# Summing the thresholds of an FP4 quantiser with separate compares and adds, two of the adds on GpSimd

## The reference

```python
scale = max(max|xb| / 6, 1e-12)          # over a block of 16 values
idx = searchsorted(_MID, |xb / scale|)   # _MID: 0.25 0.75 1.25 1.75 2.5 3.5 5.0
q = _GRID[idx] * sign(xb) * scale        # _GRID: 0 0.5 1 1.5 2 3 4 6
h = silu(xq @ wgq.T) * (xq @ wuq.T)      # 1024 -> 2816
ffn = quant(h) @ wdq.T                   # 2816 -> 1024
```

## Time and profile before

| | |
|---|---|
| median of 3 runs | 14323.8 us (14305.8 to 14346.3) |
| the profiled execution | 14373.7 us |
| its span, slowest core (core 5) | 14372.0 us |
| spans of the eight cores | 14229.1 to 14372.0 us |
| mean granted TensorE clock, cores 0 to 3, 4 to 7 | 0.652, 0.643 of full speed |
| busy on core 5: TensorE, VectorE, ScalarE, GpSimd | 45%, 51%, 18%, 10% |
| VectorE, stage 3 after its weights | busy 2979 of 4400 us |

### The profile page before, as it was taken

The page is one execution under the profiler, slowest core; times in us unless marked ns, Lnnn a source line. Parts: engine busy times, 40 slices in busy tenths (PEclk is TensorE's granted clock), DMA queues, the critical chain, the costliest instruction groups (busy, mean ns, idle before and its releaser), DMA issues.

```text
span 14372.0 us, 115863 instructions; the slowest of 8 cores (14229.1 to 14372.0 us)
## 1 busy us (share of the span) xinstructions
PE 6406.0 (45%) x27434; PEld 2691.4 (19%) x27434; DVE 7295.3 (51%) x19406; ACT 2554.8 (18%) x3860; POOL 1501.5 (10%) x1616
## 2 busy tenths in 40 slices
PE   1444444444545555554554003344334333440577
PEld 1111111111222222222221001111111111110233
DVE  4333334443444434434445986666666666668300
ACT  2222222222222222222222111111111111111000
POOL 1111111110000000000001111111111111111000
PEclk8777777776655555565555556666666666665677
DMA  2111111101100010010010000000000000001233
GB/s 61 42 42 42 37 41 39 39 34 49 46 26 28 30 42 25 28 46 26 28 46 23 30 31 11 11 21 12 11 11 22 11 11 22 11 9 37 100 111 110
DMA packets 285008, 505.41 MB, mean 35 GB/s; under 512 B 35506, under 2 KB 207410, under 8 KB 282306
## 3 DMA queue, kind: packets, MB, share of 16 engines
q1 hardware_dynamic: 235842, 333.82, 7.3%
q0 software_dynamic: 48512, 164.18, 3.0%
HBM read 294.17 MB, written 199.81 MB: 34 GB/s over the span
## 4 chain that ended last, share of the span: by engine, by line
PE 26%; issue 25%; DVE 23%; DMA 13%; ACT 9%; SPq 2%; DVEq 1%; ACTq 0%; POOL 0%; POOLq 0%
PE p_d L1603 4%; PE p_u L1480 4%; DMA s_siluz<-stg_ev 4%; DMA s_xbc<-stg_ev 4%; DVE q_s L305 3%; PE p_g L1471 2%; PE p_sc L1370 2%; ACT q_sg L257 2%; PE p_seg L1370 2%; DMA hqt<-s_hqT 2%; DVE hb L1500 1%; PE ptrA L372 1%; DVE q_s L323 1%; DVE q_amax L275 1%; ACT q_absx L256 1%
## 5 line engine op out<-in xcount | busy, mean ns | idle before, releaser
L1480 PE MATMUL p_u<-wut,xq 128*128 128x512 bf16 (+1 forms) x3072 | 842.7, 430 | 1649.1 <-DVE hb L1500 1649.1
L345 POOL TENSOR_TENSOR q_ss<-q_sg,q_sclh 128x512 f16<-128x512 f16 (+3 forms) x560 | 787.7, 1424 | 5400.3 <-DVE q_rcp L285 5200.4
L678 PE MATMUL pmm<-xhT,wnt 128*128 128x512 bf16 (+1 forms) x4352 | 1078.4, 392 | 207.8 <-ACT stg_ev L695 205.4
L305 DVE SCALAR_TENSOR_TENSOR q_s<-q_aa,q_s 128x512 f16<-128x512 f16 (+3 forms) x1680 | 975.4, 646 | 0.3 <-DVE q_s L299 0.3
L1603 PE MATMUL p_d<-wdt,hqt 128*128 128x512 bf16 x2816 | 763.8, 446 | 200.4 <-DVE ostg L1617 199.5
L1471 PE MATMUL p_g<-wgt,xq 128*128 128x512 bf16 (+1 forms) x3072 | 796.9, 409 | 26.9 <-ACT gs L1492 18.7
L1492 ACT ACTIVATE gs<-p_g 128x512 bf16<-128x512 f32 (+1 forms) x384 | 213.0, 555 | 3272.1 <-DVE hb L1500 1858.8
L724 DVE COPY dtstg<-pmm 16x512 f32<-16x512 f32 x16 | 10.8, 678 | 1437.7 <-PE pmm L683 1437.7
L1480 PEld LDWEIGHTS p_u<-wut,xq 128*128 128x128 bf16 x3072 | 337.7, 113 | 2093.4 <-issue 1863.9
L1187 DVE SCALAR_TENSOR_TENSOR attb<-eb,ldtT,scoresM 128x256 bf16<-128x256 bf16 x1024 | 455.1, 485 | 498.3 <-ACT eb L1173 428.5
L1500 DVE TENSOR_TENSOR hb<-p_u,gs 128x512 f32<-128x512 f32 (+1 forms) x384 | 246.7, 642 | 873.5 <-PE p_u L1480 873.3
(11 more groups left out here) (218 smaller groups left out, 12810.4 us busy)
## 6 DMA issues: line engine op xcount, KB each, us to landing
s_hqT<-hqTb POOLq DMA_DIRECT2D x16, 2816.0 KB, 11.5
hqt<-s_hqT SPq DMA_DIRECT2D x16, 2816.0 KB
xbcw<-s_xbc SPq DMA_DIRECT2D x272, 128.8 KB
s_xbc<-stg_ev SPq DMA_DIRECT2D x272, 128.0 KB
ubuf<-u SPq DMA_DIRECT2D x16, 2048.0 KB
s_siluz<-stg_ev POOLq DMA_DIRECT2D x256, 128.0 KB, 2.0
zld<-s_siluz SPq DMA_DIRECT2D x16, 2048.0 KB
ubp<-u SPq DMA_DIRECT2D x64, 512.0 KB
```

What stands on the lines that cost most here:

```text
L305: vop(f"t{k}", i, nc.vector.scalar_tensor_tensor(q["s1"][:, CS[i]], q["aa"][:, CS[i]], QTHR[k], q["s1"][:, CS[i]], ALU.is_gt, ALU.add))
L345: ii = nc.gpsimd.tensor_mul(q["ss"][:, CS[i]], q["sg"][:, CS[i]], q["sclh16"][:, GS[i]].unsqueeze(2) .broadcast_to([128, hb, 16]))
L678: nc.tensor.matmul(pm[0:rows, :], wnt[:, k * F + ft * 128: k * F + ft * 128 + rows], xhT[:, k * TILE:(k + 1) * TILE], start=(k == 0), stop ...
L1480: i = nc.tensor.matmul(p_u[:, 0:nn], xqb[:, k * TILE + mt * 128: k * TILE + (mt + 1) * 128], wut[:, k * FFI + i0: k * FFI + i1], start=(k ...
```

## The change

Three new scratch tiles `cd`, `c5`, `c6`. The compare-and-add instructions go: each threshold is now compared on its own (a tensor-scalar instruction, `is_gt` then a multiplication by the weight 1, 2 or 4), and added by a plain tensor-tensor add. The adds of thresholds 2 to 4 and the last one (`fin`) are on VectorE; the two that gather `s2`, `c5` and `c6` are on GpSimd, in two halves, four instructions per call. VectorE waits for them before `fin`. Also, ScalarE's `absx` and `sg` of the next call now wait for the last `aa` and the last `ss` of the call before, in place of its end.

```diff
             if q.get("prev") is not None:
-                w(scalar, "ve", q["prev"])
-                w(scalar, "gp", q["prev_gp"])
+                w(scalar, "ve", q["prev_absx"])
+                w(scalar, "gp", q["prev_sg"])
...
-            for k in (1, 2, 3):
-                for i in (0, 1):
-                    vw(mk[(f"t{k-1}", i)])
-                    vop(f"t{k}", i, nc.vector.scalar_tensor_tensor(
-                        q["s1"][:, CS[i]], q["aa"][:, CS[i]], QTHR[k],
-                        q["s1"][:, CS[i]], ALU.is_gt, ALU.add))
...
+                vop("c0", i, nc.vector.tensor_scalar(
+                    q["cc"][:, CS[i]], q["aa"][:, CS[i]], QTHR[1], 1.0,
                     ALU.is_gt, ALU.mult))
...
+                vop("t1", i, nc.vector.tensor_add(
+                    q["s1"][:, CS[i]], q["s1"][:, CS[i]], q["cc"][:, CS[i]]))
+                vop("c1", i, nc.vector.tensor_scalar(
...
+                vop("t2", i, nc.vector.tensor_add(
...
+                vop("c2", i, nc.vector.tensor_scalar(
...
+            for i in (0, 1):
+                vw(mk[("t2", i)])
+                vw(mk[("c2", i)])
+                vop("t3", i, nc.vector.tensor_add(
+                    q["s1"][:, CS[i]], q["s1"][:, CS[i]], q["cc"][:, CS[i]]))
+                vop("u0", i, nc.vector.tensor_scalar(
+                    q["s2"][:, CS[i]], q["aa"][:, CS[i]], QTHR[4], 2.0,
+                    ALU.is_gt, ALU.mult))
+                vop("u1", i, nc.vector.tensor_scalar(
+                    q["c5"][:, CS[i]], q["aa"][:, CS[i]], QTHR[5], 2.0,
+                    ALU.is_gt, ALU.mult))
+                vop("u2", i, nc.vector.tensor_scalar(
+                    q["c6"][:, CS[i]], q["aa"][:, CS[i]], QTHR[6], 4.0,
                     ALU.is_gt, ALU.mult))
             for i in (0, 1):
                 vw(mk[("t3", i)])
...
+                nc.vector.wait_ge(sems["gp"], gp_ad[i])
+                vop("fin", i, nc.vector.tensor_add(
+                    q["s1"][:, CS[i]], q["s1"][:, CS[i]], q["s2"][:, CS[i]]))
             for i in (0, 1):
-                vw(mk[("v2", i)])
-                nc.vector.wait_ge(sems["gp"], gp_ss[i])
+                vw(mk[("fin", i)])
                 vop("ds", i, nc.vector.tensor_mul(
                     dst[:, CS[i]], q["s1"][:, CS[i]], q["ss"][:, CS[i]]))
...
+            for i in (0, 1):
+                gpsimd.wait_ge(sems["ve"], mk[("u2", i)])
+                ii = nc.gpsimd.tensor_add(
+                    q["s2"][:, CS[i]], q["s2"][:, CS[i]], q["c5"][:, CS[i]])
+                inc(ii, "gp")
+            for i in (0, 1):
+                gpsimd.wait_ge(sems["gp"], gp0 + 3 + i)
+                ii = nc.gpsimd.tensor_add(
+                    q["s2"][:, CS[i]], q["s2"][:, CS[i]], q["c6"][:, CS[i]])
+                inc(ii, "gp")
```

More of the change, by code:

```diff
@@ L233, in quant_scratch @@
             "cc": sb(f"{tag}_cc", [128, n], F16 if f16 else BF16),
+            "cd": sb(f"{tag}_cd", [128, n], F16 if f16 else BF16),
+            "c5": sb(f"{tag}_c5", [128, n], F16 if f16 else BF16),
+            "c6": sb(f"{tag}_c6", [128, n], F16 if f16 else BF16),
             "ss": sb(f"{tag}_ss", [128, n], F16 if f16 else BF16),
@@ L259, in emit_quant_full @@
         AC = cnt["ac"]
-        gp_ss = [cnt["gp"] + 1, cnt["gp"] + 2]
+        gp0 = cnt["gp"]
+        gp_ss = [gp0 + 1, gp0 + 2]
+        gp_ad = [gp0 + 5, gp0 + 6]
         mk = {}
@@ L273, in _ @@
                 vw(q["prev"])
+                nc.vector.wait_ge(sems["gp"], q["prev_gp"])
             for i in (0, 1):
@@ L301, in _ @@
                     ALU.is_gt, ALU.mult))
-            for k in (1, 2, 3):
-                for i in (0, 1):
-                    vw(mk[(f"t{k-1}", i)])
-                    vop(f"t{k}", i, nc.vector.scalar_tensor_tensor(
-                        q["s1"][:, CS[i]], q["aa"][:, CS[i]], QTHR[k],
-                        q["s1"][:, CS[i]], ALU.is_gt, ALU.add))
-            for i in (0, 1):
-                vop("u0", i, nc.vector.tensor_scalar(
-                    q["s2"][:, CS[i]], q["aa"][:, CS[i]], QTHR[4], 1.0,
+                vop("c0", i, nc.vector.tensor_scalar(
+                    q["cc"][:, CS[i]], q["aa"][:, CS[i]], QTHR[1], 1.0,
@@ L311, in _ @@
                     ALU.is_gt, ALU.mult))
             for i in (0, 1):
[L313 to L318, removed]
+                vw(mk[("t0", i)])
+                vw(mk[("c0", i)])
+                vop("t1", i, nc.vector.tensor_add(
+                    q["s1"][:, CS[i]], q["s1"][:, CS[i]], q["cc"][:, CS[i]]))
@@ new lines, in _ @@
+                vop("c1", i, nc.vector.tensor_scalar(
+                    q["cd"][:, CS[i]], q["aa"][:, CS[i]], QTHR[2], 1.0,
+                    ALU.is_gt, ALU.mult))
+            for i in (0, 1):
+                vw(mk[("t1", i)])
+                vw(mk[("c1", i)])
+                vop("t2", i, nc.vector.tensor_add(
+                    q["s1"][:, CS[i]], q["s1"][:, CS[i]], q["cd"][:, CS[i]]))
+                vop("c2", i, nc.vector.tensor_scalar(
+                    q["cc"][:, CS[i]], q["aa"][:, CS[i]], QTHR[3], 1.0,
+                    ALU.is_gt, ALU.mult))
@@ L349, in _ @@
                 inc(ii, "gp")
-        assert cnt["gp"] == gp_ss[1]
+            for i in (0, 1):
[3 more added lines that the diff above has]
+                inc(ii, "gp")
+            for i in (0, 1):
+                gpsimd.wait_ge(sems["gp"], gp0 + 3 + i)
+                ii = nc.gpsimd.tensor_add(
+                    q["s2"][:, CS[i]], q["s2"][:, CS[i]], q["c6"][:, CS[i]])
+                inc(ii, "gp")
+        assert cnt["gp"] == gp0 + 6
         q["prev"] = cnt["ve"]
         q["prev_gp"] = cnt["gp"]
+        q["prev_absx"] = mk[("aa", 1)]
+        q["prev_sg"] = gp_ss[1]
         return cnt["ve"]
```

## The result

The changed kernel takes 14743.4 us (median of 8 runs, 14711.4 to 14787.0), the kernel before beside it 14334.7: ratio 1.0288, 95% interval 1.0266 to 1.0309. That is slower by 409 us; the forecast was +387 us, 2.7%, in a range of 14480 to 15020.

A forecast was written before the change was run, and what follows sets the result against it. Bound: one chain through VectorE, 324 quantisation calls in full. Calls +444 us and ScalarE's earlier release -57 give +387, on a 14324 us median: 14711 us, range 14480 to 15020.

The forecast's parts named there:

- One chain through VectorE: Quantisation calls: waits in stage 3 are for work VectorE itself releases, so all 324 calls count in full.
- Rival D: The call's growth is partly covered, for instance by TensorE in stages 1 and 3; half covered 14490; chance 0.05.
- The saving: VectorE, each f16 call: 8.0 us removed, 5.1 added; alone saves 2.9 us, about 740 us over 256 calls.
- T: 1,024-column f16 call: when the first half's `u2` is done, forecast 3.56 us from the first L305's old place.
- the mark: Zero point for timing a call: where the first L305, a compare, stood in the old order.
- The wait: VectorE held by GpSimd's adds before `fin`; f16 call 9.93 against 8.77 us, +1.15; narrow +1.10, weight +2.25.
- The price of an add: GpSimd add taken as 1.05 us for 512 columns, 0.83 for 384; bounds 0.95 to 1.22.
- Whoever waits gets in as the other ends: Turn-taking of VectorE and GpSimd instructions that don't overlap, read from the earlier trace; GpSimd's add enters after `t3`.
- Rival A: VectorE and GpSimd do overlap: +0.39 us per f16 call, +1.07 per f32, 14440 in all; chance 0.05.
- rival C: A plain GpSimd add is much cheaper than a product with a broadcast operand; at 0.60 us 14153; chance 0.03.
- rival B: Each GpSimd add lasts 1.49 us: +545 us more, 15256; chance 0.05.
- The release: ScalarE released earlier: VectorE waits less in stage 1 and the weight stages, nothing in stage 3; together -57 us.

The follow-up runs named there:

- first experiment: The changed kernel with the four GpSimd adds of each call moved to VectorE; 0.9712 of the kernel before.
- extra-adds run: Kernel with all adds on VectorE, plus four GpSimd adds per f16 call into an unread scratch tile; 1.0342 of the kernel before, against 0.9712 without them.
- reordered one: The changed kernel with the three high-threshold compares (u0, u1, u2) moved in front of the low ones; 1.0203 of the kernel before.
- two-adds run: The changed kernel with two of the four GpSimd adds of a call (those of c6) moved to VectorE; 1.0005 of the kernel before.

## Why the prediction was right

**The bound.** One chain through VectorE, every call in full: stage 3 grew by 239 us. The calls as measured there give 128x1.36+64x1.13 = 246, so hardly anything was covered (on core 3 VectorE's wait for `p_u` fell from 870.6 to 849.2 us). Rival D is out.

**The saving.** The pitches held: compare 0.20, plain add 0.335 (starts at 11208.37 and 11208.70). T, the end of the first half's `u2`, came 3.57 us behind the mark, 3.56 forecast. The first experiment shows the saving without GpSimd: 0.9712, 0.968 expected.

**The wait.** From T to the end of the call 6.56 us, 6.37 forecast; the call +1.36 against +1.15; the narrow call +1.13 (11247.61 to 11255.68) against +1.10; the weight call 11.74 us (8321.10 to 8332.84) against 11.55, +2.44 where 2.25 was forecast. In these two the mark is again set behind the start of the first compare as in the old order (0.99 and 1.52 us); for the weight call, by its first compare and its products:

```profile
8319.58 1.27 DVE L305 TENSOR_SCALAR qw_s<-qw_aa 128x512 bf16<-128x512 f32 x1
...
8332.09 0.75 DVE L348 TENSOR_TENSOR wbf<-qw_s,qw_ss 128x512 bf16<-128x512 bf16 x2
```

**Two steps in it were off.** The price of an add was taken as 1.05 and measured 1.14 us (0.83 and 0.90 for 384 columns), within the bounds that I gave (0.95 to 1.22). The last three adds run from 11210.36 to 11213.72, 3.36 us in place of 3.15, and that is all of the 0.19 us. And the order at T was not the one chosen. I had GpSimd get in after `t3` and hold the second half's compares until T+1.78. In the trace they run freely to T+0.94, and GpSimd's first add, started at T+0.14, ends only at T+1.94, some 1.0 us behind the last of them. That is one of the prediction's own signs of being wrong ("if `t3` and the compares don't get held"), and the other order that it named and priced at 0.1 us. It was worth almost nothing: GpSimd's second add starts at T+1.91, T+1.93 forecast (T+1.49 and 1.56 in the narrow call, T+2.31 and 2.34 in the weight call), since in either order the compares and the add stand one behind the other. VectorE's idle time before `fin` is 3.32 us in place of about 2 for the same reason. "Whoever waits gets in as the other ends" is not general. It is what happens in the extra-adds run and in the reordered one, but not behind this `t3`, nor in the two-adds run, where GpSimd waits through six VectorE instructions. What decides who gets in first was not settled.

**Exclusion.** Argued from the earlier trace rows, shown by the experiments from the reordering on. Rival A (14440) and rival C fell with them and with the first; rival B's 1.49 us is not the work of an add: L370, with VectorE out of the way, has a mean of 1143 ns, and only L365, whose first add has to wait, one of 1469.

**The release.** -57 us forecast, 52 less idle time in the trace, 27 +/- 29 us by the runs: compatible with both. The share of it in stage 1 (12.7 us less idle time) does not show in the length of that stage.

**The sum.** With the measured calls it would be 192x1.36+64x1.13+68x2.44-52 = +447 us. The lengths of the stages bear that out (us, median of the eight cores in the two traces):

| | before | after | growth | forecast |
|---|---|---|---|---|
| stage 1, first block maximum to last product | 2896.4 | 2979.9 | 83.5 | 61 |
| gate and up weights, first block maximum to first `hb` | 788.5 | 883.7 | 95.2 | 89 |
| stage 3, first to last `hb` | 4346.1 | 4584.9 | 238.8 | 218 |
| down weights, first block maximum to last product | 408.8 | 432.3 | 23.5 | 20 |

That is 441 us where 388 was forecast: every stage grew by more than its forecast, by 53 us together. The runs' medians differ by 409 (interval 381 to 443). They are times of the slowest core, and which core that is hangs in part on the down projection, which the change leaves alone and which took 885 to 977 us on the cores before and 881 to 967 after; in the two profiled executions the slowest core grew by 379 us and the median core by 444. So 387 came nearer to 409 than its steps deserved, and that part is luck. The 32 us between 441 and 409 have no cause that I tested.

## What to carry to other kernels

Moving elementwise work from VectorE to GpSimd did not relieve VectorE here: each GpSimd add took some 0.9 us out of VectorE's time, waited for or not, while the same work on VectorE was 0.335 us for an add and 0.60 for a product. This held beside tensor-scalar, tensor-tensor and scalar-tensor-tensor instructions; no trace here has a reduction, a reciprocal or a read of PSUM beside a GpSimd instruction, so for those it is not shown. So look for a VectorE instruction several times its usual length beside a GpSimd row, and price GpSimd work on VectorE's chain. In f16 a compare-and-add of 0.60 us is worth splitting into a compare of 0.20 and an add of 0.335, when the adds stay on VectorE; with an f32 input the compare is 0.335 too, and the split of one such instruction gains nothing.

## What the runs showed of the hardware

- GpSimd's elementwise instructions exclude VectorE's for a whole instruction: a 32-column one went from 0.16 to 0.93 us, 512-column compares from 0.28 to 1.23, a plain add from 0.41 to 1.36. It holds with no data and no semaphore between the two within the call, and at nearly the full price, 0.88 us for each add that nobody waited for.
- It holds for a scalar-tensor-tensor too: in stage 2 of the kernel before, L1187 (256 columns, bf16) has a median of 482 ns and takes up to 850 when it starts less than 0.1 us behind a GpSimd product (L1288, 612 ns).
- The exclusion is not fair in every case: a GpSimd add that had started stayed out for 0.80 us behind four short VectorE instructions, and for some 1.5 us behind six, while in other places it got in at once. What decides it is not shown.
- A GpSimd add of two contiguous f16 operands takes 1143 ns for 512 columns and 902 for 384; the product with a broadcast operand took 1.05 us when alone.
- A dependent VectorE add or product of 1,024 f16 columns directly behind its producer started 0.79 to 0.86 us after it, an independent one of the same size 0.61.
